# First query step of each pair moved beside the last key tiles, 52 query slots after it instead of 56

## The reference

```
q, k = elu(t @ wq.T + b) + 1, elu(t @ wk.T + b) + 1 ;  v = t @ wv.T + b
kv_cos = einsum('bshx,bshz->bhxz', k*cos, v) ;  kv_sin = the same with k*sin
qkv   = einsum(q*cos, kv_cos) + einsum(q*sin, kv_sin)
denom = 1 / (q*cos . sum_s(k*cos) + q*sin . sum_s(k*sin) + 1e-5)
t = t + (qkv * denom) @ dense.T + b ;  t = t + ffn(layernorm(t))
```

## Time and profile before

| | |
|---|---|
| median of 3 runs | 3526.32 us (3520.82 to 3526.87) |
| time of the profiled execution | 3529.31 us |
| its span, first to last instruction | 3527.5 us, mean granted clock 0.982 |
| PE busy | 3191.5 us (90%) |
| DVE busy | 2415.9 us (68%) |
| ACT busy | 1975.6 us (56%) |
| POOL busy | 1968.3 us (56%) |

### The profile page before, as it was taken

How to read it: one execution, slowest core, us unless ns; L and a number is a source line. 1 busy time by engine, 2 the same in 40 slices (tenths; PEclk the granted TensorE clock), 3 DMA queues, 4 the chain that set the end, 5 groups by cost and what they waited for, 6 DMA issues and landing times.

```text
span 3527.5 us, 44913 instructions
## 1 busy us (share of the span) xinstructions
PE 3191.5 (90%) x17092; PEld 1488.6 (42%) x17092; DVE 2415.9 (68%) x2773; ACT 1975.6 (56%) x2209; POOL 1968.3 (56%) x1303
## 2 busy tenths in 40 slices
PE   3898999989899998989989898998989999899977
PEld 2543345434443335433454344443354333543333
DVE  5887766967668676776668666686756866645754
ACT  1166654766556764666646665476645676444430
POOL 1167861878428882478727785297833888121320
PEclk8999999999999999999999999999999999999988
DMA  2002740046300661016510363005620075202678
GB/s 55 19 1 57 156 104 28 1 98 146 82 19 0 145 143 56 1 29 152 133 31 0 80 152 85 28 1 125 141 60 19 2 161 135 52 1 65 149 169 279
DMA packets 69297, 278.75 MB, mean 79 GB/s; under 512 B 30845, under 2 KB 35485, under 8 KB 64221
## 3 DMA queue, kind: packets, MB, share of 16 engines
q1 hardware_dynamic: 69085, 275.89, 32.5%
HBM read 242.78 MB, written 33.05 MB: 78 GB/s over the span
## 4 chain that ended last, share of the span: by engine, by line
PE 72%; DVE 11%; ACT 7%; DMA 5%; issue 4%; SPq 1%; POOL 0%; DVEq 0%; ACTq 0%; POOLq 0%
PE ps_D L1590 15%; PE ps_C L1523 10%; PE ps_A L1508 5%; PE ps_B L1508 5%; PE ps_D L1523 5%; PE ps_E L1568 5%; PE ps_E L1523 5%; PE ps_B L1552 3%; PE ps_D L1366 3%; PE ps_A L1552 3%; DVE region L1149 2%; PE ps_A L1385 2%; DMA RB<-r_keep 2%; DVE arena L1000 2%; DMA r_keep<-RR 2%
## 5 line engine op out<-in xcount | busy, mean ns | idle before, releaser
L610 POOL TENSOR_TENSOR arena<-arena,UHL 128x896 f32<-128x896 f32 x525 | 1106.6, 2112 | 252.8 <-ACT UHL L771 252.6
L1590 PE MATMUL ps_D<-region,small 128*128 128x448 f32 x1792 | 759.3, 550 | 9.7 <-DVE OS L1185 6.6
L592 POOL TENSOR_TENSOR region<-region,RB 128x896 f32<-128x896 f32 x224 | 468.9, 2093 | 174.9 <-DMA RB<-r_keep 174.5
L771 ACT ACTIVATE UHL<-arena,W8C 128x896 f32<-128x896 f32 x525 | 540.9, 1033 | 0.4
L620 POOL TENSOR_TENSOR UA<-region,CS 128x128 f32<-128x128 f32 (+1 forms) x400 | 224.6, 563 | 449.4 <-PE ps_C L1523 401.3
L1590 PEld LDWEIGHTS ps_D<-region,small 128*128 128x128 f32 x1792 | 322.9, 190 | 291.8 <-issue 237.8
L815 ACT ACTIVATE EQ<-ps_B,NEG 128x896 f32<-128x896 f32 x224 | 225.5, 1007 | 361.4 <-PE ps_B L1552 361.4
L1523 PE MATMUL ps_C<-region,UA 128*128 128x512 f32 (+1 forms) x800 | 382.5, 601 | 18.1 <-ACT region L689 18.1
L1000 DVE SCALAR_TENSOR_TENSOR arena<-arena,W8C 128x448 f32<-128x448 f32 (+1 forms) x235 | 358.3, 1545 | 0.0
L1158 DVE TENSOR_TENSOR region<-region,ps_C 128x896 f32<-128x896 f32 x224 | 242.9, 1084 | 142.3 <-ACT ps_C L779 142.0
L1125 DVE SCALAR_TENSOR_TENSOR region<-region,ps_A 128x1024 f32<-128x1024 f32 (+1 forms) x200 | 242.6, 1213 | 140.2 <-ACT region L797 140.2
(11 more groups left out here) (308 smaller groups left out, 4983.8 us busy)
## 6 DMA issues: line engine op xcount, KB each, us to landing
RB<-r_keep SPq DMA_DIRECT2D x448, 448.0 KB, 6.0
arena<-x SPq DMA_DIRECT2D x8, 1568.0 KB, 6.6
t_keep<-Y SPq DMA_DIRECT2D x7, 1568.0 KB, 5.2
r_keep<-RR SPq DMA_DIRECT2D x448, 7.0 KB, 2.9
w_keep<-region SPq DMA_DIRECT2D x7, 784.0 KB, 5.5
arena<-w_keep SPq DMA_DIRECT2D x4, 784.0 KB, 10.6
arena<-L_ffn_weight SPq DMA_DIRECT2D x1, 2080.0 KB
CST<-cst SPq DMA_DIRECT2D x1, 1568.0 KB, 6.4
```

The lines of the kernel that those rows point to most:

```text
L592: pool.tensor_tensor(out=q, in0=q, in1=RB[:, cc].rearrange("p (c n) -> p c n", c=2), op=ALU.mult).then_inc(pool_scaled.sem, 1)
L610: pool.tensor_tensor(out=X[:, cut], in0=X[:, cut], in1=PRODUCT[m % 3], op=ALU.add).then_inc(pool_taps.sem, 1)
L771: act.activation(PRODUCT[m % 3].rearrange("p (h w) -> p h w", w=W), g_window(2 * g * ROWS + 2 * (k // 5), 2 * (k % 5) - 4, 2 * ROWS), ACT. ...
L1590: ins = pe.matmul(here.area(key)[:, 0:PIX], MW[i][:, c, :], Q[s % 3][:, c, :], start=c == 0, stop=c == NCHUNK - 1)
```

## The change

Step 0 of each pair leaves the query slots. Its four projections go into key tiles 33, 35, 37 and 39 (`FIRST_TILES`), its denominators behind tile 41's products, its sum into tile 43; before them image 0's head matrices go into tiles 29 and 31. All of these use area C in turn, which is free once image 0's sums are copied out. PE issues each of them between `k_project(k)` and `k_products(k-2)`, but the denominators behind the latter. DVE does the copies and features in the next tile, behind that tile's `k_features`. Step 0's features lie in `QFIRST`: three pieces of `un2` and one `SQ`, buffers of the second norm. In eight tiles (`NO_PIECE`) DVE does no depthwise piece; tiles 44 to 49 now have one, and two pieces are left for slots 12 and 15. For chunks 0 and 2 of step 0 DVE multiplies by RB in SBUF (`first_scale`), not by a copy in PSUM.

Steps 1 to 13 follow in 52 slots. Chunk 0 of step 1 is projected in the key part's last round, image 1's head matrices come in slots 1 and 3, and step 0's outputs in slots 2, 4, 6 and 8. The lags of the other steps stay. The 45 tap products that lie in slots come four in five slots from slot 1 on, not three in four from slot 3 on. Cut to its core:

```diff
-K_PIECES, FRONT_PIECES, Q_PIECES, DRAIN_PIECES = 1, PIECES, (1, 0, 0, 1), 1
-PRODUCT_TILE, PRODUCT_SLOT, POOL_LAG, DRAIN_SLOT = 20, 3, 4, 64
+FRONT_PIECES, Q_PIECES, DRAIN_PIECES = PIECES, (1, 0, 0, 1), 1
+HEAD_TILES, FIRST_TILES, FIRST_DEN, FIRST_SUM = (29, 31), (33, 35, 37, 39), 41, 43
+NO_PIECE = (30, 32, 34, 36, 38, 40, 42, 43)
+PRODUCT_TILE, PRODUCT_SLOT, POOL_LAG, PIECE_SLOT, DRAIN_SLOT = 20, 1, 1, 12, 60
-PRODUCT_SLOTS = {PRODUCT_SLOT + n + n // 3: n for n in range(POOL_PIECES - TILE_PRODUCTS)}
-SLOTS = 4 * STEPS
+PRODUCT_SLOTS = {PRODUCT_SLOT + n + n // 4: n for n in range(POOL_PIECES - TILE_PRODUCTS)}
+SLOTS = 4 * (STEPS - 1)
+HEAD_SLOTS = (1, 3)
+FIRST_OUT_SLOTS = {2: 0, 4: 1, 6: 2, 8: 3}
+FIRST_POOL_SLOTS, FIRST_PARTS_SLOT = {0: 1, 2: 3}, 10
+        QFIRST = [un2[:, i * 2 * PIX:(i + 1) * 2 * PIX] for i in range(3)]
+        QFIRST += [SQ[:, :, :].rearrange("p g c -> p (g c)")]
...
+                uses += [(("m", 0, HEAD_TILES.index(k)), "C")] if k in HEAD_TILES else []
+                uses += [(("qp", 0, FIRST_TILES.index(k)), "C")] if k in FIRST_TILES else []
+                uses += [(("den", 0), "C")] if k == FIRST_DEN else []
+                uses += [(("dsum", 0), "C")] if k == FIRST_SUM else []
```

SP, before the loads of RB for step 1, and GpSimd, in the slots:

```diff
+                        if s == 1:
+                            sp.wait_ge(*first_scaled.at(pair, h + 1))
+                            sp.wait_ge(*scaled_by_pool(pair, 0, 2 * h + 1))
...
+                    if j in FIRST_POOL_SLOTS:
+                        pool_scale(here, 0, FIRST_POOL_SLOTS[j])
```

ScalarE, in the key tiles and at slot 0:

```diff
+                    if k in FIRST_TILES:
+                        q_exponential(here, 0, FIRST_TILES.index(k))
-                products_out(here, 1)
...
+                        q_exponential(here, *chunk_of(j))
+                    if j == 0:
+                        products_out(here, 1)
```

VectorE, in key tile `k` behind `k_features(k)`, in the slots, and its new function:

```diff
-                    if conv and k > NORM_TILE:
-                        depthwise(here, pair + 1, K_PIECES, DVE_PIECES)
-                for i in range(2):
-                    head_matrices(here, i)
+                    if k - 1 in HEAD_TILES:
+                        head_matrices(here, 0, HEAD_TILES.index(k - 1))
+                    if k - 1 in FIRST_TILES:
+                        q_features(here, 0, FIRST_TILES.index(k - 1))
+                    if k == FIRST_DEN + 1:
+                        den_parts(here, 0)
+                    if k == FIRST_SUM:
+                        den_guard(here, 0)
+                        den_reciprocal(here, 0)
+                    if conv and k > NORM_TILE and k not in NO_PIECE:
+                        depthwise(here, pair + 1, 1, DVE_PIECES)
+                first_scale(here, 0)
                 for j in range(ALL_SLOTS):
+                    if j == FIRST_PARTS_SLOT:
+                        out_parts(here, 0)
                     if 1 <= j <= SLOTS:
-                        q_features(here, *divmod(j - 1, 4))
+                        q_features(here, *chunk_of(j - 1))
+                    if j - 1 in HEAD_SLOTS:
+                        head_matrices(here, 1, HEAD_SLOTS.index(j - 1))
+                    if j == 1:
+                        first_scale(here, 2)
...
+            def first_scale(here, cc):
+                q = features(0, cc)
+                dve.wait_ge(*spread_loaded[cc // 2].at(here.pair, 1))
+                dve.tensor_tensor(out=q, in0=q, in1=RB[:, cc].rearrange("p (c n) -> p c n", c=2),
+                                  op=ALU.mult).then_inc(first_scaled.sem, 1)
```

TensorE, in the key tiles, then in the slots:

```diff
                     if k < KTILES:
                         k_project(here, k)
+                    if k in HEAD_TILES:
+                        head_matrices(here, 0, HEAD_TILES.index(k))
+                    if k in FIRST_TILES:
+                        q_project(here, 0, FIRST_TILES.index(k))
+                    if k == FIRST_SUM:
+                        q_sums(here, 0)
+                    if k == KTILES + 1:
+                        q_project(here, 1, 0)
...
                     if k >= 2:
                         k_products(here, k - 2)
+                    if k == FIRST_DEN:
+                        for g in range(2):
+                            q_denominators(here, 0, g)
...
+                    if 1 <= j < SLOTS:
+                        q_project(here, *chunk_of(j))
+                    if j in HEAD_SLOTS:
+                        head_matrices(here, 1, HEAD_SLOTS.index(j))
...
+                    if j in FIRST_OUT_SLOTS:
+                        q_output(here, 0, FIRST_OUT_SLOTS[j])
```

More of the change, by code:

```diff
@@ L587, in pool_scale @@
             def pool_scale(here, s, cc):
-                q = Q[s % 3][:, 2 * cc:2 * cc + 2, :]
+                q = features(s, cc)
                 pool.wait_ge(*here.emptied(("qp", s, cc)))
@@ L676, in tokens @@
                     act.wait_ge(*square_free)
+                if which == 2 and g == 0:
+                    act.wait_ge(*here.filled(("out", 0)))
                 src = here.area(key)[:, 0:m * P].rearrange("p (t c) -> p t c", c=P)
@@ L789, in products_out, with q_exponential @@
                         .then_inc(*here.empty(key))
+            def q_exponential(here, s, cc):
+                key = ("qp", s, cc)
+                act.wait_ge(*here.filled(key))
+                act.activation(EQ[:, cc % 2], here.area(key)[:, :].rearrange("p (c n) -> p c n", c=2)[:, :, 0:PIX],
+                               ACT.Exp, bias=NEG1[:, 0:1]).then_inc(eq_ready.sem, 1)
             def pair_of_images(here):
@@ L1529, in k_products, with head_matrices @@
                     ins.then_inc(kv_used.sem, 1)
-            def head_matrices(here, i):
-                for b in range(1 + i):
-                    pe.wait_ge(*here.emptied(("kv", i, b)))
-                for g in range(2):
-                    key = ("m", i, g)
-                    pe.wait_ge(*here.room(key))
-                    for h in range(8 * g, 8 * g + 8):
-                        c = h // 2 % 4
-                        half = slice(h % 2 * C, (h % 2 + 1) * C)
-                        ins = pe.matmul(here.area(key)[half, c * 256:c * 256 + P + 2],
-                                        AT[i][:, h * C:(h + 1) * C], BD[:, h, :], start=True, stop=True)
-                    ins.then_inc(*here.fill(key))
+            def head_matrices(here, i, g):
+                key = ("m", i, g)
+                if g == 0:
+                    for b in range(1 + i):
+                        pe.wait_ge(*here.emptied(("kv", i, b)))
+                pe.wait_ge(*here.room(key))
+                for h in range(8 * g, 8 * g + 8):
+                    c = h // 2 % 4
+                    half = slice(h % 2 * C, (h % 2 + 1) * C)
+                    ins = pe.matmul(here.area(key)[half, c * 256:c * 256 + P + 2],
+                                    AT[i][:, h * C:(h + 1) * C], BD[:, h, :], start=True, stop=True)
+                ins.then_inc(*here.fill(key))
             def q_project(here, s, cc):
@@ L1587, in q_output @@
                 pe.wait_ge(*(scaled_by_pool(here.pair, s, cc) if cc in POOL_SCALED
-                             else here.emptied(("rb", s, cc))))
+                             else here.emptied(("rb", s, cc)) if s else first_scaled.at(here.pair, cc // 2 + 1)))
                 for c in (2 * cc, 2 * cc + 1):
-                    ins = pe.matmul(here.area(key)[:, 0:PIX], MW[i][:, c, :], Q[s % 3][:, c, :],
+                    ins = pe.matmul(here.area(key)[:, 0:PIX], MW[i][:, c, :], features(s, cc)[:, c % 2, :],
                                     start=c == 0, stop=c == NCHUNK - 1)
```

108 lines of the change are left out of this document (55 added, 53 removed).

## The result

The changed kernel takes 3554.18 us (median of 4 runs, 3552.16 to 3555.82), the kernel before 3526.6 beside it (4 runs, 3520.82 to 3534.48): a ratio of 1.0076 [1.0056, 1.0097], 28 us slower. The forecast was 3531 in a range from 3497 to 3550. The profiled execution's span is 3553.5 us, against 3527.5 before.

The account below looks back on a forecast made before the run. The prediction took PE's work as the floor. Idle time of +1.2 us in seven loop pairs and -0.6 in the last gave +7.8, less 2.6 for the clock: about +5 on the median 3526.3, so 3531 us, range 3497 to 3550.

Parts of the forecast that it names:

- the floor: Whole pair: PE's work is the floor and its total doesn't change; the change is worth the difference of PE's idle times.
- the key part: Key tiles: PE waits at moved items 6.7 us in a loop pair, 5.3 in the last; about 11 us longer.
- R1: Rival, faster: the waits in the key tiles are not there; 3482 in full, 3506 with half gone; chance 0.3 together.
- (a): Key tiles 30 to 46 before the change: PE waits 0.21 us a tile for DVE, 3.4 us in all, forecast to go.
- the last pair: Last pair's key tiles and first slots: 8.9 us of PE idle time after the change against 9.5 before, so -0.6.
- the hand layout of the slots: Slots 0 to 10: 21.0 us of work, 7.6 idle (last pair 3.6); slot 11 begins 28.6 us after the last product.
- the price of DVE beside POOL: Turn and first slots: `first_scale` costs 1.08 us at best, about 3.1 beside a just begun POOL instruction; 2.0 to 3.0 taken.
- R2: Rival, slower: each DVE instruction with two SBUF inputs waits for a whole POOL instruction; +3 us a loop pair, 3552; chance 0.15.
- the term for the clock: First slots: denser slots should have fewer spells at the lower clock level, two of about 1.3 us each: -2.6 us.
- slots 12 and 15: Slots 12 and 15: a depthwise piece each on DVE makes one projection wait 1.8 us (bounds 0 and 3.5).
- the slot pieces' term: The depthwise pieces in slots 12 and 15: one projection waits 1.8 us in a loop pair.

Follow-up runs that it names:

- e4: The changed kernel with PE issuing the key tiles' moved items behind the products, and ACT's exponential of a moved chunk a tile later: 3503.62 us.
- e5: The changed kernel with the edits of e1 and e4 together: 3436.99 us, ratio 0.9744 against the kernel before.
- e1: The changed kernel with both POOL multiplies of step 0 moved later, to slots 3 and 7 instead of 0 and 2: 3485.9 us.
- e2: The changed kernel without the depthwise piece in tile 49, which is done in a later slot: 3540.81 us.
- e8: The changed kernel with one added wait: in loop pairs POOL waits for ACT's first slot product before its first multiply of step 0: 3486.28 us.
- e3: The changed kernel with only the second POOL multiply of step 0 moved later, to slot 7 instead of 2: 3514.03 us.

## Why the prediction was wrong, step by step

*Right: the floor and the key part.* PE's idle time is what the change moves, and the moved items wait in front of ready products. I had 6.7 us of waits in a loop pair and 5.3 in the last, and a key part 11 us longer; e4 took the waits away and found 6.7 and 6.0, and the part is 11.7 us longer. Single waits came out at 0.88 where I had 1.0, and 1.80 where I had 2.4; for the sum of tile 43 I had 0.4 and none is seen, so PE idles 5.8 us there in pair 3 and not 6.7. R1, that these waits are not there, is refuted. The waits of (a) are gone too: in e5, where nothing else waits, PE idles 0.2 us from tile 29 to P.

*Right: the last pair.* I had -0.6, it is -0.9 in the stretches that the change touches. There is no row on POOL in it, and the hand layout of the slots holds: with 3.6 us of waits slot 11 was to begin 21.0 + 3.6 = 24.6 us after P, and it begins 24.8 after it. In e1, which is free of the row in loop pairs too, it begins at 1571.25 - 1546.13 = 25.1. One sign failed: `first_scale` was to be near 1.1 us long here, and it is 2.20, as POOL was not free. It ends 0.95 us behind the one multiply beside it, which is the price that I had for one instruction.

*Wrong: the price of DVE beside POOL, in the turn, and the clock behind it.* The step that failed reads: "`first_scale` costs 1.08 at best and about 3.1 if POOL (2.09 us an instruction) has just begun." From the earlier trace rows, one DVE instruction beside one POOL instruction, I took the end of that one instruction as the longest wait, 2.0 to 3.0 us for `first_scale`, and nothing at all for tile 49's piece. I had written down, one sentence later, that two multiplies and the first sums follow back to back, and did not ask what the wait is in such a row. Measured are 5.81 for the piece and 2.95 for `first_scale` in six of the loop pairs. In the seventh, pair 4, the piece got through and `first_scale` took the whole row:

```profile
1988.70 9.44 DVE L1201 TENSOR_TENSOR un<-un,RB 128x896 f32<-128x896 f32 x1
```

PE's wait for projection (1,2) was 5.54 us and not 2.2, and the clock's lower level took about 3 more: from 1576.39 to 1582.50 PE did work of half that time. Some of it came back in waits that then weren't there: from P to slot 11 PE idled 33.2 - 24.9 = 8.3 us in pair 3, and I had 7.6. That this sum is nearly right is luck, since it stands in one long wait and not in many short ones. PE was busy 24.9 us in that stretch, and 22.1 in e1 at full clock, so 2.8 of the lost time are the clock, for which the first slots of my sum had nothing; the waits alone are 0.7 over mine. (The other 1.1 between 24.9 and my 21.0 is that records reach past the next start; e1 has them too.) Slot 11 began 1602.18 - 1568.95 = 33.2 us after P, not 28.6, so the term is 4.6 us too small there; by slot 12 it is 4.2 on average (35.7 us after P, before 31.5), 29 us over seven pairs. R2 named this mechanism, on this side, but priced it with the same single instruction: 3552 at 0.15. That 3552 is near 3554 is luck: R2 has +3 us a pair from waits of one instruction each, and its sign, over 12 us of idle time in slots 0 to 15, isn't there (9.5 in pair 3).

*Wrong: the term for the clock.* I took 2.6 us off for denser slots. In place of that each loop pair got a slow spell, behind its stall, of the 2.8 us above.

*Covered: slots 12 and 15.* I had 1.8 us. The step from slot 12 to slot 16 takes 12.2 to 12.9 us in loop pairs and 11.6 in the last, so 0.6 to 1.3 more; but the kernel before has such losses there as well. From slot 12 to the last chunk it is 138.9 us on average before, 127.1 after, and the four slots' 11.6 us taken off leaves -0.2. Outside of all these stretches (before tile 29, behind the last chunk) a loop pair is 0.7 us shorter. With the measured sizes it is 11.7 (key part) - 11.6 (four slots) + 4.2 (first slots) - 0.2 - 0.7 = +3.4 us, and the pairs show the same.

Without the row, my own sum would have had 3.6 and not 7.6 us of waits in the first slots of a loop pair: 1.2 - 4.0 = -2.8 a pair, so 3531 - 28 = 3503. Slot 12 in e1 bears out the 4.0: 27.6 us after P on average, 3.9 less than before. But e1 is 3485.9 and its loop pair 5.9 us shorter than before, where the sum has 2.8. Of the difference 1.9 are the slot pieces' term, and 2.0 lie outside the stretches that the change touches (182.0 us where before has 184.0); against them 0.8 of the forecast's gain in the key part and the first slots didn't come, which leaves the missing 3.1. Of the 2.0 some 1.6 are the clock. The start of a loop pair up to tile 29 takes 81.10 us at a granted clock of 1.00 and 82.76 at 0.98; before, five of the seven are of the longer kind, in e1 two. Behind the last chunk four pairs before have a clock of 0.97 or 0.98 (102.0 to 103.9 us, else 100.6), in e1 one. What makes these spells come in one pair and not in another stays open, and the change was not made for them.

## What to carry to other kernels

Where a DVE instruction with two SBUF inputs is on the path, look at POOL's timeline there for gaps, not for its share of busy time (11.62 of 23.00 us in the earlier trace rows told nothing): what it may cost is the length of the whole row of POOL instructions that it starts beside, and one pause in that row, even a wait put in by hand, can be worth more than the work that it delays. In an engine that works in order, put an item that may wait behind the ready ones, not ahead of them; price a new stall with the slow clock that may follow it.

## What the runs showed of the hardware

**A row on POOL shuts DVE out as a whole, and slows POOL hardly at all.** In the row of the changed kernel POOL's instructions keep 2.07 to 2.08 us each while DVE's piece stands for 5.81. The one ahead of which DVE's gets in is longer, 2.44 and, in e2, 2.93 us. So the two don't run at half speed beside each other here; one works or the other. (The Trainium skill, Trainium Architecture — The Big Picture, What this means for kernel authors, calls the contention for the ports that the two share an exclusive lock and not a bandwidth split. These rows agree; how long one side may keep it, the page doesn't say.)

**Not every border of two POOL instructions keeps DVE out.** In the key tiles POOL goes from a tap sum to `UA` without a gap, and DVE's piece gets in there: 1.73 us, 0.49 after the sum. At the turn it is shut out from tap sum to multiply and from multiply to multiply, gets in from a multiply to the tap sum in six of the seven pairs, here and in e2, and in pair 4 doesn't get in there either, nor from `UA` to a tap sum. What decides it stays open. Whether POOL's next instruction was ready in time does not: in pair 4 its product was ready 0.8 us ahead, and DVE was kept out; at the fold's instruction before the change it had been ready for 3.8, and DVE got in.

**A stall of 5.54 us cost the clock.** Behind it PE's matmuls take 0.58 us and not 0.36 for about 6 us (the lower of the two levels; granted clock 0.52 from 1576.30 to 1582.60), in each loop pair of the changed kernel and of e4, and at that place in none of e1 and e8, where there is no such stall. Behind e2's stall of 3.1 to 3.2 us the first matmul takes 0.36 in five pairs and 0.55 in one, and behind e3's of 1.6 to 1.7 us 0.36 in all seven. Behind its wait of 1.87 us in the kernel before the first matmul takes 0.36.
